# Three steps between the four parts of a projection, and 36 steps a batch for those of the first stage

## The reference, cut to what matters

```python
# x is (4, 1024, 128) float32, 16 heads of 8 dimensions
x = x + 0.5 * ffn(layernorm(x))
x = x + attention(layernorm(x)) # softmax(q k^T * scale + relative position bias) v, then w_proj and b_proj
x = x + 0.5 * ffn(layernorm(x))

def ffn(x):
    x = x + msa(layernorm(x)) # attention over the same 1024 tokens, no bias
    return x + moe(layernorm(x)) # each token through the one of 8 experts that its gate picks, 128 -> 512 -> 128
```

## Time and profile before

| what | value |
| --- | --- |
| median of 3 timed executions | 2452.49 us (2449.7 to 2457.5) |
| profiled execution, its own time | 2455.49 us |
| its span, first to last instruction | 2453.7 us |
| mean granted TensorE clock | 0.928 of full speed |
| TensorE, VectorE, ScalarE, GpSimd busy | 87%, 79%, 78%, 31% |

### The profile page before, as it was taken

How to read it: one execution, slowest core, us unless ns; L and a number is a source line. 1 busy time by engine, 2 the same in 40 slices (tenths; PEclk the granted TensorE clock), 3 DMA queues, 4 the chain that set the end, 5 groups by cost and what they waited for, 6 DMA issues and landing times. The chain is left out here.

```text
span 2453.7 us, 59789 instructions
## 1 busy us (share of the span) xinstructions
PE 2142.3 (87%) x22882; PEld 767.4 (31%) x22882; DVE 1934.2 (79%) x3219; ACT 1909.3 (78%) x3561; POOL 771.6 (31%) x1167
## 2 busy tenths in 40 slices
PE   5898988889987999999899999899888888988935
PEld 1222222225421323542233233222222223532425
DVE  7988899885788896578888898899989997569210
ACT  1788798789877777788778778788979888878822
POOL 1343533330634622032442032022161232062153
PEclk7899799899989999999999899999999999989967
DMA  4234422135304334642442332111101103622525
GB/s 112 79 90 123 119 61 71 44 97 161 79 24 102 97 99 128 198 124 69 112 110 80 93 93 80 44 32 43 29 20 42 37 20 104 186 48 61 141 81 145
DMA packets 265568, 213.37 MB, mean 87 GB/s; under 512 B 64241, under 2 KB 219761, under 8 KB 265250
## 3 DMA queue, kind: packets, MB, share of 16 engines
q1 hardware_dynamic: 254018, 201.15, 29.5%
q0 software_dynamic: 11264, 8.40, 1.9%
HBM read 159.62 MB, written 59.77 MB: 89 GB/s over the span
## 5 line engine op out<-in xcount | busy, mean ns | idle before, releaser
L1301 ACT ACTIVATE probs<-psum 128x512 f32<-128x512 f32 x3072 | 1619.5, 600 | 302.0 <-PE psum L1068 184.0
L1414 DVE TENSOR_REDUCE maxes<-psum 128x2 f32<-128x1024 f32 x1216 | 1421.9, 1217 | 248.7 <-PE psum L1036 238.2
L1105 PE MATMUL psum<-probs,v_ones 128*9 128x256 f32 (+1 forms) x11520 | 990.0, 417 | 0.0
L1068 PE MATMUL psum<-q_staged,k_staged 27*128 27x512 f16 x3072 | 803.3, 404 | 50.5 <-DMA q_staged<-neg_max 19.8
L1036 PE MATMUL psum<-k_staged,q_staged 24*128 24x512 f16 x3072 | 628.3, 407 | 161.1 <-DVE maxes L1414 124.3
L1419 DVE CUSTOM_DVE_ANT_0 biased<-psum,strips 128x512 bf16<-128x512 f32 x640 | 408.9, 686 | 94.5 <-PE psum L1036 77.9
L1036 PEld LDWEIGHTS psum<-k_staged,q_staged 24*128 24x128 f16 x3072 | 145.4, 91 | 900.5 <-DVE maxes L1414 514.2
L1068 PEld LDWEIGHTS psum<-q_staged,k_staged 27*128 27x128 f16 x3072 | 221.2, 91 | 174.6 <-ACT probs L1301 80.2
L1105 PEld LDWEIGHTS psum<-probs,v_ones 128*9 128x9 f32 x11520 | 171.9, 89 | 330.2 <-issue 232.6
L817 POOL TENSOR_SCALAR max_rest<-max_turned 128x32 f32<-128x32 f32 x96 | 28.4, 296 | 657.9 <-DVE max_turned L1457 655.7
L815 POOL TENSOR_SCALAR max_rest<-max_turned,far_bias_rows 128x32 f32<-128x32 f32 x32 | 13.0, 406 | 353.6 <-DVE max_turned L1457 353.3
(11 more groups left out here) (167 smaller groups left out, 1278.0 us busy)
## 6 DMA issues: line engine op xcount, KB each, us to landing
m_w<-in_w SPq DMA_DIRECT2D x204, 256.0 KB
near<-bias_near SPq DMA_DIRECT2D x128, 160.0 KB
strips<-bias_strips SPq DMA_DIRECT2D x64, 288.0 KB, 3.2
k_staged<-k_parts SPq DMA_DIRECT2D x192, 48.0 KB
heads<-heads_t SPq DMA_DIRECT2D x384, 18.0 KB
m_y<-sorted_tokens SPq DMA_DIRECT2D x34, 192.0 KB
expert_out<-m_out SPq DMA_DIRECT2D x34, 192.0 KB, 3.2
q_staged<-q_parts SPq DMA_DIRECT2D x128, 48.0 KB
```

The costliest lines, as they stand in the source:

```text
L1068: mm_ = pe.matmul(bank[:, :], k.kst[p][rows_, kt * P:(kt + 1) * P], queries, start=True, stop=not biased_)
L1105: last = pe.matmul(heads_bank[32 * j:32 * j + VC, columns], k.v[:, batch_of(u) * KT + kt, u % QUADS * 4 + j, :], probs[:, step % 3 * 4 + j ...
L1301: act.activation(probs[:, step % 3 * 4 + e % 4, :], bank[:, :], ACT.Exp, scale=unscale[is_mid(u)]).then_inc(taken, 1)
L1414: dve.reduce_max(maxes[u % 2][:, half, 2 * i:2 * i + 2, t, chunk], slot, AX.X).then_inc(drained, 1)
```

## The change

The parts of a projection go from 0, 2, 3 and 4 steps behind its step to 0, 3, 6 and 9; the split goes from 5 to 7 and the store from 9 to 11. The projection steps themselves move too:

| projections | before | after |
| --- | --- | --- |
| stage 0, batches 1, 2, 3 (h = 0 and 1) | 9, 17; 25, 33; 41, 49 | 9, 21; 45, 57; 81, 93 |
| stage 1, batches 0 to 3 | 221, 227; 253, 259; 349, 355; 381, 387 | 217, 229; 249, 261; 345, 357; 377, 389 |
| stage 2, batches 0 to 3 | 403, 411; 467, 475; 531, 539; 595, 603 | 405, 417; 469, 481; 533, 545; 597, 609 |

Statistics and norms stay 9 and 7 steps ahead and so move with them; the loads of units 16 and 24 go from steps 238 and 366 to 242 and 370. The gathers, outputs, expert work and unit loads stay where they are. No instruction is added or removed. The first two projections (0, 0, h) run ahead of step 0 and are untouched.

```diff
     if n == 0:
-        return 8 * ((b - 1) * 2 + h) + 9
+        return 36 * (b - 1) + 12 * h + 9
     if n == 1:
-        return gather_step(0, b) + 6 * h + 18
-    return output_step(1, b, 1) + 8 * h + 72
+        return gather_step(0, b) + 12 * h + 14
+    return output_step(1, b, 1) + 12 * h + 74
...
-PROJECT_SINCE = {0: "p_turn", 2: "p_q", 3: "p_k", 4: "p_v"}
-SPLIT_SINCE, STORE_SINCE = 5, 9
+PROJECT_SINCE = {0: "p_turn", 3: "p_q", 6: "p_k", 9: "p_v"}
+SPLIT_SINCE, STORE_SINCE = 7, 11
```

## The result

The changed kernel takes 2472.94 us (median of 4, 2469.05 to 2473.63), the kernel before 2453.88 in the same session (median of 4, 2449.70 to 2457.50): a ratio of 1.0076, 95% interval 1.0055 to 1.0097. It is slower by some 19 us; 2453 was forecast, and the range up to 2466 does not hold it.

What follows compares the result with a forecast made beforehand. VectorE was taken to bound plain steps, no engine to be full in crowded ones, and TensorE to be fuller in stage 1. Gains of 25 us met costs of 25, so 2453 us, no change, range 2439 to 2466.

Steps and rivals of the forecast that it cites:

- Gain 16: 12 projections in stages 0, 1 and 2: spread parts at 0.29 us each gain 1.4 us a projection; 16 us (9 to 24).
- Gain 4: Stage 2's batches 0 and 1, lying in stage 1: spread parts gain 1.9 us a batch; 4 us (0 to 9).
- it does nothing: Rival: lone parts cost as much as crowded ones, 0.8 each; 2453 to 2458 us; chance 0.45 shared with the sum's no change.
- Step 208, "Cost 3.5": Stage 1, batch 0: VectorE's early statistics wait 8.7 us for the gathers, mostly overlapped; cost 3.5 us (2 to 6).
- Step 240, "cost 5.5": Stage 1, batch 1: statistics wait 7.5 us for gathers, in series with unit 16's later load; cost 5.5 us (3 to 9).
- Step 336, "cost 3.5": Stage 1, batch 2: VectorE's statistics wait 4.9 us for the gathers; cost 3.5 us (2 to 5).
- Step 368, "cost 5.5": Stage 1, batch 3: statistics wait 5.2 us for gathers, then unit 24's load some 6 us later; cost 5.5 us (3 to 9).
- For the other six projections of stage 1 ... 0: Stage 1, batches 1 to 3: lost places ahead of the carry at t = 8 cancel the distance's gain; 0 (3 either way).
- Step 74, "Cost 4": Norm of (0, 3, 0) on GpSimd delays the split of the maxima 5.5 us, against 1.2 slack; cost 4 us (2 to 5.5).
- Gain 5: Step 591: the norm leaves step 588, so VectorE's 4.06 us wait for the output's add goes; 5 us (4 to 7).
- Cost 3: TensorE, everywhere: idle in the longer waits leaves it at half clock afterwards; cost 3 us (0 to 8).
- the early statistics win: Rival: gather waits at steps 208, 240, 336 and 368, in series with unit loads, cost over 26 us; 2464; chance 0.18.

Runs made afterwards that it cites:

- experiment 5: Changed kernel with the old distances (0, 2, 3, 4; split 5, store 9) in stage 0 alone, at the new steps: 2472.66 us, ratio 1.0084.
- experiment 4: Changed kernel, stage 1 statistics 5 and norms 3 steps ahead, with stage 1's old part distances at the new places: 2457.55 us, ratio 1.0035.
- experiment 7: Kernel before with stage 2 alone changed, places and distances: 2449.64 us, ratio 0.9983; new places with old distances: 2453.35 us, ratio 1.0004.
- early statistics alone: Kernel before with stage 1's statistics 13 steps ahead instead of 9, norms left at 7: 2462.05 us, ratio 1.0048.
- both edits: Kernel before with stage 1's statistics 13 steps ahead and loads of units 16 and 24 at steps 242 and 370: 2472.16 us, ratio 1.0087.
- experiment 3: Kernel before, stage 1 edits: late loads 2456.02 us; statistics and norms four steps earlier 2503.57; statistics alone earlier 2462.05; these with late loads 2472.16.
- experiment 6: Changed kernel with the GpSimd norm of projection (0, 3, 0) issued at step 73 instead of 74: 2467.27 us, ratio 1.0063.

## Why the prediction was wrong

The waits were foreseen; the step that failed is the sum's sizes, and they failed to one side. The largest failure is in "Gain 16" and "Gain 4", with the price of 0.29 us for a lone part: the runs give 3 to 5 us for stages 0 and 2 together, where the terms make 18. For stage 1 the terms make a cost of 15, and the runs give 21 to 25. (The clock's 3 us, a term by itself in the sum, are inside both measured figures.) Term by term, with the table's rows beside them:

- **"A lone part so costs 0.29 us", "Gain 16": mis-sized.** The rows of after give 0.74 for q, k or v, and adjacent parts cost 0.72 (experiment 5). The part was priced with VectorE's slack, from an output projection's row; where a lone part stands every three steps TensorE is 96% busy. The distance does give something in places: up to 3.5 us over four projections of stage 0, which the wait for the next carry took back (experiment 5), and 2 to 3 us at two sites of stage 1 against some 3 lost at another (experiment 4). In stage 2 it gave 5.6 in steps 528 to 623 (247.4 less 241.8, the mean of the eight traces), as forecast, but that is in good part luck: about half of it is a collision on GpSimd that it avoids (experiment 7). The last rival, "it does nothing", had the price of a part right at 0.8.
- **"Gain 4"** for stage 2's batches 0 and 1: 1.3 in this pair of traces, and nothing that stands clear of the differences between traces.
- **Step 208, "Cost 3.5"**: right, or a little low. Step 209 takes 12.51 and not 2.48 us, and most of it is overlapped by the idle time of the earlier trace rows; steps 208 to 239 are 4.5 and 4.8 longer with the early statistics alone and with both edits (experiment 3).
- **Step 240, "cost 5.5"**: right in the place (4.7), in each wait, and in the two being in series (experiment 3).
- **Step 336, "cost 3.5": mis-sized, 7.4.** The wait is the 4.90 forecast, with 1.26 of statistics behind it. I took 1.24 and some more back for later in the unit. Steps 341 and 342 give 1.0 back, but step 338, right behind the stall, is at half clock and takes 1.7 more (its windows before and after follow), and step 343 takes 1.1 more, since TensorE now waits 1.76 us and not 0.67 for the next carry. The run with early statistics alone has 6.3 here.

```profile
1097.21:1100.25 3.04, 3.04 (x44) 0.82 (x44) 2.17 (x7) 2.17 (x5) 0.00 (x0) 1.00 0.50 100
...
1105.83:1110.60 4.77, 4.77 (x44) 0.80 (x43) 2.60 (x9) 2.17 (x5) 2.33 (x3) 0.54 0.18 50
```

```profile
1113.22 0.39 PE L1068 MATMUL psum<-q_staged,k_staged 27*128 27x512 f16 x2 [0.67 <-DMA q_staged<-neg_max]
...
1123.64 0.45 PE L1068 MATMUL psum<-q_staged,k_staged 27*128 27x512 f16 x2 [1.76 <-DMA q_staged<-neg_max]
```

- **Step 368, "cost 5.5": mis-sized, 8.7,** with a wait of 6.29 for 5.2 and the load behind it.
- **"For the other six projections of stage 1 ... 0": wrong, some 3 us for batch 2.** I saw that the old parts lay ahead of the wait for the carry at t = 8 and took that as something the distance would have to beat. It was the cover of that wait. Taken away, it uncovered the wait, and the part moved behind it was done at half clock. Of the 4.3 in the table 1.1 are step 367, which takes 2.8 to 5.7 us in kernels with stage 1 as before; the close parts at the same place lose under 1 (experiment 4).
- **Step 74, "Cost 4"**: the norm did delay the carry, for 4.85 us of TensorE; steps 76 and 79 alone hold 6.3. Taking it out gives 6.6 us by step 80 and 3.2 by step 208, near the 4 that I had (experiment 6).
- **"Gain 5" at step 591**: the wait went, and steps 592 to 596 are 4.0 shorter. It is kept only with the wide distance; with the close parts as much is lost by step 623 (experiment 7). Unit 37 is 7.8 shorter, 2.3 of it lost in the next unit, to which the second projection has moved.
- **"Cost 3" for the clock**: not to be measured by itself. The granted clock over the span went from 0.928 to 0.925; the slow stretches are inside the terms above, at each stall. The Trainium skill (TensorE: Matmul & The Clock Gate, "HAM oscillation") has such cold matmuls behind a wait for a DMA, and the rows at 1172.03 and 1175.06 agree.

Of the rivals, "the early statistics win" is the one that came true: it was to decide from 26 us at the four sites on, and by the table their stretches hold 20.8 (4.7, 7.4, 8.7, without the first) to 24.4 (with it), so it did not pass its own mark; it decided because the gains were not there to pay for it. The rival's own time, 2464, has all the gains in it. With these at their lower bounds (9 + 0 + 4 and not 25) and the four sites at their upper ones (29 and not 18) the sum is 2476, above the result. I kept the dear part and the dear waits apart as different cases when both could hold at once, and so the range ended at 2466.

Open: what part of steps 256 to 335 the wide distance makes good (-3.9 in the table, 1 to 3 of it the trace of before, the rest 2 to 3 by experiment 4, one trace against another); why steps 368 to 383 cost 8.7 in the changed kernel and 3.0 with the two edits of experiment 3, beyond the longer wait; and how far the distance and how far the collision make the gain in steps 528 to 623.

## What to carry to other kernels

An in-order engine that is asked for something a few steps early stands still for all that is queued behind it; look for the next queue that paces itself by the stalled work, since what that queue issues comes late as well, and the two come in series (at the sites of the loads here 2.7 and 1.0 us one by one, 7.3 together).

Work ahead of a fixed latency is its cover. Before moving it, ask which wait ends behind it; after the move the wait is bare, and the moved work may run at the lower clock. The other way round, time gained ahead of such a wait can be lost in it: 3.5 us at step 74 were none at step 80.

A gain that shows early in the trace may be work put off: compare at a step where both kernels have done the same. And before a row of such a table is explained, see how much the same steps differ between traces of kernels that don't differ there; here it was up to 3 us. Price an added operation by the engine that it fills, not by the one that was the bound without it.

## What the runs showed of the chip that I had not expected

TensorE's clock was already halved when it came out of a wait of 2.48 us for the carried maxima: the same eight products took 1.04 us and not 0.62, the same q part 2.08 and not 1.12, and the first matmul at full length again (0.39) is 6.5 us after the wait. What it had done before the wait was one part and plain steps, at clock 1.00. The length of the wait alone doesn't tell it. Behind the 2.08 us at the end of step 607 (experiment 7) the first pair of score matmuls still took 0.39 us, and 0.61 from 1.97 us after the wait on. Behind the 0.67 us at 1113.22 in the kernel before, a pair took 0.61 us 0.97 us later; over the step with that wait TensorE was busy 2.24 of 3.37 us.
